# A twelve-stage decoder kernel: the two-way attention stage is written anew, with the gate weights folded into the value weights

## What is computed

```
Q_char = x @ Wq_c.T + bq_c;   K_sub  = ctx @ Wk_s.T + bk_s;  V_sub  = ctx @ Wv_s.T + bv_s
char2sub = softmax(Q_char @ K_sub.T / sqrt(128)) @ V_sub
Q_sub  = ctx @ Wq_s.T + bq_s; K_char = x @ Wk_c.T + bk_c;    V_char = x @ Wv_c.T + bv_c
sub2char = softmax(Q_sub @ K_char.T / sqrt(128)) @ V_char
gate = sigmoid(concat(char2sub, sub2char) @ Wg.T + bg)
out  = gate * char2sub + (1 - gate) * sub2char
```

## Time and profile before

| | |
|---|---|
| three runs, median (lowest to highest) | 1545.04 us (1542.69 to 1550.32) |
| the profiled execution: its own time, its span | 1544.58 us, 1542.8 us |
| mean granted TensorE clock, whole span | 0.947 |
| TwoWay with its LayerEnd | 177.2 to 245.6 us of the span |
| granted clock in that stretch | 0.83 |

### The profile page before, as it was taken

How to read it: one execution, slowest core, us unless ns; L and a number is a source line. 1 busy time by engine, 2 the same in 40 slices (tenths; PEclk the granted TensorE clock), 3 DMA queues, 4 the chain that set the end, 5 groups by cost and what they waited for, 6 DMA issues and landing times.

```text
span 1542.8 us, 24060 instructions
## 1 busy us (share of the span) xinstructions
PE 1311.6 (85%) x8965; PEld 835.4 (54%) x9015; DVE 942.9 (61%) x2189; ACT 668.5 (43%) x1896; POOL 398.4 (26%) x326
## 2 busy tenths in 40 slices
PE   7999866887877788777987379899898999999997
PEld 4666653555655533324564345556565666566664
DVE  2556566776665589986756867555764555633334
ACT  4555322556565486633642036322244555422222
POOL 1333102543432168835100252000101333300000
PEclk9999978999999998879998699999999999999999
DMA  9000000000000055520002200000000000000000
GB/s 392 3 1 2 0 1 1 1 1 1 1 1 1 21 129 126 127 59 2 2 1 96 124 1 2 1 1 0 1 2 1 1 1 1 1 1 1 0 0 14
DMA packets 13260, 43.29 MB, mean 28 GB/s; under 512 B 1760, under 2 KB 3936, under 8 KB 12512
## 3 DMA queue, kind: packets, MB, share of 16 engines
q1 hardware_dynamic: 13152, 41.84, 8.5%
HBM read 41.19 MB, written 0.66 MB: 27 GB/s over the span
## 4 chain that ended last, share of the span: by engine, by line
PE 67%; DVE 18%; ACT 6%; issue 4%; POOL 3%; DMA 1%; DVEq 0%; SPq 0%; POOLq 0%; ACTq 0%
PE PS L1071 6%; PE PS L641 6%; PE PS L1056 5%; PE PS L1057 5%; PE PS L325 4%; DVE PS L2120 4%; PE PS L357 3%; PE PS L337 3%; PE PS L707 3%; PE PS L298 2%; PE PS L306 2%; PE PS L366 2%; PE PS L300 2%; DVE arena L2127 2%; PE PS L319 2%
## 5 line engine op out<-in xcount | busy, mean ns | idle before, releaser
L549 POOL TENSOR_TENSOR arena<-arena,small 128x768 f32<-128x768 f32 (+1 forms) x64 | 107.7, 1683 | 226.5 <-DVE small L492 117.6
L877 DVE TENSOR_REDUCE arena<-PS 128x2 f32<-128x512 f32 (+1 forms) x192 | 108.8, 609 | 53.5 <-PE PS L635 52.4
L804 ACT ACTIVATE arena<-PS 128x512 f32<-128x512 f32 (+1 forms) x192 | 92.2, 532 | 107.2 <-PE PS L641 107.2
L1160 DVE TENSOR_TENSOR arena<-arena,PS 128x512 f32<-128x512 f32 x82 | 56.4, 687 | 115.9 <-ACT arena L1093 115.8
L1093 ACT ACTIVATE arena<-PS 128x512 f32<-128x512 f32 x82 | 49.0, 597 | 166.0 <-PE PS L1057 166.0
L1927 PE MATMUL PS<-arena,w_consts 128*128 128x512 f32 x128 | 84.7, 751 | 32.7 <-DVE arena L2127 29.4
L429 ACT ACTIVATE arena<-PS,small 128x256 f32<-128x256 f32 (+1 forms) x256 | 110.6, 452 | 0.0
L641 PE MATMUL PS<-arena 32*128 32x256 f32 (+1 forms) x768 | 97.5, 370 | 13.9 <-DVE arena L877 9.3
L635 PE MATMUL PS<-arena 32*128 32x256 f32 (+1 forms) x768 | 94.6, 371 | 2.4 <-DVE arena L877 1.6
L500 DVE COPY arena<-PS 128x768 f32<-128x768 f32 (+1 forms) x64 | 69.5, 1086 | 34.6 <-PE PS L337 34.5
L2171 POOL TENSOR_TENSOR arena<-arena 128x512 f32<-128x512 f32 x64 | 80.3, 1269 | 36.6 <-DVE PS L2120 28.1
(11 more groups left out here) (398 smaller groups left out, 3019.4 us busy)
## 6 DMA issues: line engine op xcount, KB each, us to landing
arena<-rows SPq DMA_DIRECT2D x32, 512.0 KB, 4.9
w_last<-in_last SPq DMA_DIRECT2D x1, 8260.0 KB, 22.3
w_rest<-in_rest SPq DMA_DIRECT2D x1, 6463.5 KB, 38.0
w_last<-in_first SPq DMA_DIRECT2D x1, 4532.5 KB, 21.5
w_last<-in_first SPq DMA_DIRECT2D x1, 2176.0 KB, 10.4
w_last<-in_mid SPq DMA_DIRECT2D x1, 768.0 KB, 4.3
X<-in_x SPq DMA_DIRECT2D x1, 512.0 KB, 4.7
CT<-in_ctxT SPq DMA_DIRECT2D x1, 512.0 KB, 11.0
```

The costliest lines, as they stand in the source:

```text
L549: g.tensor_tensor(p, p, ri, ALU.mult).then_inc(self.pn_done.sem, 1)
L804: a.activation(self.PT[:, q % 8, :], PS[:, 3 + q % 3, 0:2 * n], ACT.Exp).then_inc(self.e_done.sem, 1)
L877: v.tensor_reduce(dst, src, AX.X, ALU.max, negate=True).then_inc(self.mx_done.sem, 1)
```

## The change

TwoWay is rewritten, and its LayerEnd works in two groups:

- The value weights of direction i get 128 more columns, the product of the value weights and the direction's half of the gate weights; five small matmuls at the stage's start make this product and the matching bias (L1493 to L1497 of the changed kernel), and ACT copies them behind the plain value weights (L1508, L1509). Each value row then carries 256 numbers: value and gate share. So the matmul with the gate weights, the copy of outputs for it and its bias in each batch go.
- The transposed weights are now the stationary operand and the values the moving one, so the outputs have tokens on partitions (L1574: 8 matmuls of 256 columns in place of 4). The transposes of the result go.
- The weights stay undivided. ACT scales direction 1's output by 1/sum as it copies it (L1633), DVE scales direction 0's in the step that adds or subtracts the two (L1671). The division of 256 x 256 weights goes.
- Queries, keys and values read CT and XT themselves; the copies to CB and XB go. One direction's source makes its queries and keys into one bank, and ACT adds the bias to both (L1517, L1518). ACT in place of DVE copies the transposed weights (L1621).
- All four batches are written out, with no hardware loop.
- `early=True`: six tiles are normed between batch 2 and the last mixing step of batch 3; 8 + 5 filler matmuls stand on PE in place of 14.
- The fields `led` and `lead` are never set, so the branches on them do nothing: `lead_tensor` and `lead_scalar` run at the stage's start.
- The stage's weights take 0.4 MB more in the second of the two loads of the "first" weights.

```diff
-    def __init__(self, c, w, bq, bk, bv, wg, nbg):
+    def __init__(self, c, wq, wk, wv, wvt, bq, bk, bv, bvc, wg, bg):
...
+    def projections(self, pe, b, ctx, bank):
+        own = c.CT if ctx else c.XT
+        src = own[:, b * S:(b + 1) * S]
+        pe.matmul(c.PS[:, bank, 0:256], self.wq[:, i, :], src, start=True, stop=True)
+        pe.matmul(c.PS[:, bank, 256:512], self.wk[:, 1 - i, :], src, start=True, stop=True)\
+            .then_inc(self.qk_done.sem, 1)
+    def lead_tensor(self, pe):
+        c.wait_weights(pe, self)
+        for i in range(2):
+            pe.matmul(PS[:, 4, i * P:(i + 1) * P], self.wvt[:, i, :], self.wg[:, i, :], start=True, stop=True)
+        pe.matmul(PS[:, 4, 256:384], self.bvc[:, 0:1].to_broadcast([P, P]), self.wg[:, 0, :], start=True, stop=False,
+        pe.matmul(PS[:, 4, 256:384], self.bg.to_broadcast([P, P]), c.ident, start=False, stop=True, skip_group_check=True)
+        pe.matmul(PS[:, 4, 384:512], self.bvc[:, 1:2].to_broadcast([P, P]), self.wg[:, 1, :], start=True, stop=True,
+        self.projections(pe, 0, True, 2)
+        pe.wait_ge(self.x_ready.sem, self.x_ready.at(0, 1 if self.led else 2))
+        self.projections(pe, 0, False, 5)
...
+        def outputs(b):
+            pe.wait_ge(self.v_ev.sem, self.v_ev.at(b, 2))
+            if b:
+                pe.wait_ge(self.d_ready.sem, self.d_ready.at(b - 1, 1))
+            pe.wait_ge(self.pt_ev.sem, self.pt_ev.at(b, 2))
+            for i in (1, 0):
+                for t in range(2):
+                    for kt in range(2):
+                        ins = pe.matmul(PS[:, 6 + i, t * 256:t * 256 + 256],
+                                        self.PT[:, i, kt * 256 + t * P:kt * 256 + t * P + P],
+                                        self.V[b % 2][:, i, kt, :], start=(kt == 0), stop=(kt == 1), skip_group_check=True)
+                ins.then_inc(self.o_done.sem, 1)
+        values_of(0)
+        scores(0)
+        queries_keys(1)
+        values_of(1)
+        for b in range(B):
+            turns(b)
+            if b + 1 < B:
+                scores(b + 1)
+            else:
+                keep_warm(c, pe, 4, 4)
+            if b + 2 < B:
+                queries_keys(b + 2)
+            outputs(b)
+            if b + 2 < B:
+                values_of(b + 2)
+        self.end.transposes(pe, 0)
+        keep_warm(c, pe, 4, 8)
...
+        def batch(b):
             for i in range(2):
+                a.wait_ge(self.t_done.sem, self.t_done.at(b, i + 1))
+                if b and i == 0:
+                    a.wait_ge(self.o_done.sem, self.o_done.at(b - 1, 2))
+                a.activation(self.PT[:, i, :], PS[:, i, :], ACT.Copy).then_inc(self.pt_ev.sem, 1)
...
+                if b + 1 < B:
+                    exps(b + 1, i)
+                if b + 2 < B:
+                    queries_keys(b + 2, i)
+            if b + 1 == B:
+                self.end.root(a, 0)
+            a.wait_ge(self.o_done.sem, self.o_done.at(b, 1))
...
+                ins = a.activation(self.BG[:, t, :], PS[:, 7, t * 256:t * 256 + 256], ACT.Copy,
+                                   scale=self.ri[b % 2][:, 1, t:t + 1])
+            ins.then_inc(self.b_ready.sem, 1)
+            a.wait_ge(self.d_ready.sem, self.d_ready.at(b, 1))
+            a.activation(self.G, self.DG[:, :, P:2 * P], ACT.Exp, scale=-1.0).then_inc(self.g_exp.sem, 1)
...
+        def mixed(b):
+            r = self.ri[b % 2]
+            v.wait_ge(self.b_ready.sem, self.b_ready.at(b, 1))
+            v.wait_ge(self.o_done.sem, self.o_done.at(b, 2))
+            for lo, op in ((P, ALU.add), (0, ALU.subtract)):
+                for t in range(2):
+                    ins = v.scalar_tensor_tensor(self.DG[:, t, lo:lo + P], PS[:, 6, t * 256 + lo:t * 256 + lo + P],
+                                                 r[:, 0, t:t + 1], self.BG[:, t, lo:lo + P], ALU.mult, op)
+            ins.then_inc(self.d_ready.sem, 1)
...
+        for b in range(B):
+            if b + 1 < B:
+                maxima(b + 1)
+            if b:
+                finish(b - 1)
+            if b + 1 == B:
+                self.end.early_stats(v)
+                self.end.tiles(v, 0)
+            mixed(b)
+            if b + 2 < B:
+                values_of(b + 2)
+            if b + 1 < B:
+                sums(b + 1)
+            gates(b)
+        finish(B - 1)
...
-            s.end = LayerEnd(c, s.z_ready, last=i == len(names) - 1, early=isinstance(s, (Attention, NarrowAttention, LocalLayers, Mamba, BitLinear)),
+            s.end = LayerEnd(c, s.z_ready, last=i == len(names) - 1, early=isinstance(s, (Attention, NarrowAttention, LocalLayers, Mamba, BitLinear, TwoWay)),
```

More of the change, by code:

```diff
@@ L226, in scalar @@
         self.root(a, g)
+        if self.lead:
+            self.lead.lead_scalar(a)
         if self.turned:
@@ L232, in tensor @@
         if self.turned:
-            keep_warm(self.c, pe, self.spare, 5 if len(self.groups) == 2 else 14)
+            if self.lead:
+                self.lead.lead_tensor(pe)
+            else:
+                keep_warm(self.c, pe, self.spare, 5 if len(self.groups) == 2 else 14)
             self.transposes(pe, len(self.groups) - 1)
@@ L1502, in values_of @@
                 for t in range(2):
[L1503 to L1512, removed]
+                    ins = pe.matmul(PS[:, 2 + i, t * 256:t * 256 + 256], self.Q[:, i, t * P:(t + 1) * P],
@@ L1568, in source, with exps @@
-        def source(it, d):
-            if d:
-                a.wait_ge(self.v_done.sem, self.v_done.at(it, 2, d - 1))
-            a.activation(self.CB, c.CT[:, bass.ds(it * S + d * S, S)], ACT.Copy)
-            a.activation(self.XB, c.XT[:, bass.ds(it * S + d * S, S)], ACT.Copy).then_inc(self.src_ready.sem, 1)
-        def keys(it, d):
+        if not self.led:
+            self.lead_scalar(a)
+        def exps(b, i):
+            a.wait_ge(self.mx_done.sem, self.mx_done.at(b, i + 1))
+            if b and i == 0:
+                a.wait_ge(self.t_done.sem, self.t_done.at(b - 1, 2))
+            for t in range(2):
+                ins = a.activation(self.Pr[:, i, t * 256:t * 256 + 256], PS[:, 2 + i, t * 256:t * 256 + 256], ACT.Exp,
+                                   bias=self.nm[:, i, t:t + 1], scale=1.0, accum_out=self.ss[:, i, t:t + 1])
+            ins.then_inc(self.e_done.sem, 1)
@@ L1581, in batch @@
             for i in range(2):
-                a.wait_ge(self.mx_done.sem, self.mx_done.at(it, i + 1))
-                for t in range(2):
-                    ins = a.activation(self.Pr[:, i, t * 256:t * 256 + 256], PS[:, 6 + i, t * 256:t * 256 + 256],
-                                       ACT.Exp, bias=self.nm[:, i, t:t + 1], scale=1.0,
-                                       accum_out=self.ss[:, i, t:t + 1])
-                ins.then_inc(self.e_done.sem, 1)
-            if more:
-                keys(it, 1)
@@ new lines, in batch @@
+            for t in range(2):
+                ins = a.activation(self.BG[:, t, :], PS[:, 7, t * 256:t * 256 + 256], ACT.Copy,
[3 more added lines that the diff above has]
+            a.activation(self.G, self.DG[:, :, P:2 * P], ACT.Exp, scale=-1.0).then_inc(self.g_exp.sem, 1)
+        exps(0, 0)
+        queries_keys(1, 0)
+        exps(0, 1)
+        queries_keys(1, 1)
@@ L1607, in vector @@
+        for b in range(B):
+            batch(b)
     def vector(self, v):
@@ new lines, in finish, with sums @@
+            v.tensor_tensor(c.Z[:, 2 * b:2 * b + 2, :], self.G, self.BX, ALU.add).then_inc(self.z_ready.sem, 1)
+        def sums(b):
+            v.wait_ge(self.e_done.sem, self.e_done.at(b, 2))
+            link(v.reciprocal(self.ri[b % 2], self.ss))
+        values_of(0)
+        maxima(0)
+        values_of(1)
+        sums(0)
+        for b in range(B):
+            if b + 1 < B:
+                maxima(b + 1)
+            if b:
+                finish(b - 1)
[5 more added lines that the diff above has]
+                values_of(b + 2)
+            if b + 1 < B:
+                sums(b + 1)
+            gates(b)
```

256 lines of the change are left out of this document (103 added, 153 removed).

## The result

| | before | after |
|---|---|---|
| median of seven runs each | 1545.04 us (1542.15 to 1551.02) | 1534.6 us (1532.63 to 1537.06) |
| profiled execution: own time, span | 1544.58, 1542.8 | 1536.69, 1534.6 |
| x ready behind TwoWay | 245.56 | 231.28 |

The ratio of the times is 0.9929, 95% interval 0.9907 to 0.9951: 10.4 us faster by the medians, 7.6 to 14.4 by the interval. The forecast was 1533, its range 1529 to 1540.

A forecast was written before the change was run, and what follows sets the result against it. A ring of dependent steps was taken as TwoWay's bound, PE after the change. x ready at 233.5 instead of 245.56 saves 12.0 us: span 1530.8, execution 1532.6, plus 0.46 for the median: 1533, range 1529 to 1540.

The forecast's parts named there:

- The ring and its end: In TwoWay, PE bounds batches 0 and 1 at 9.55 us each, and batch 2's outputs end at 216.0.
- The slack of 1.2 us: In each batch, PE has 4.35 us of work while DVE and ACT need about 3.1 to copy the weights.
- The sixteen weight loads at nothing: In each batch's outputs, weight loads cost nothing, each lying under the 0.21 us record before it.
- The start: At TwoWay's start, clock at 1.2 GHz until about 181.1, 0.85 us a matmul, values starting at about 183.5.
- rival 3: More gain: clock up already at 177.4 (1.9 us less), 1 us less in hand-overs; gain 15, 1530; chance 0.07.
- The repeated-column matmuls at 0.22 each: At TwoWay's start, they cost as any 128-column matmul; at worst as 256 columns, +1.3 us for three.
- The tail: From batch 2's outputs at 216.0, DVE bounds TwoWay's end, and x is ready at 233.5.
- about 1.4 on this item alone: In TwoWay's tail, six early tiles add 4.5 us to the path and replace 6.7 by 3.6 behind the last sum.
- The price weighed: For mixing in four steps of 128 numbers, the profile row's 1.12 us was used over the skill's estimate of 1.03.
- Its like would take 1532.6: Whole kernel: a profiled execution like the one of 1544.58 us would take 1532.6, with span 1530.8.
- Rival 2: Clock takes part back: 1.2 GHz stretches at L0f's start and in the PE-bound part; gain 6.7, 1538; chance 0.20.
- L0f longer by more than 2 us: A sign that the prediction is wrong: the stage behind TwoWay grows by more than 2 us.

The follow-up runs named there:

- after_scores_twice: Changed kernel with the four score matmuls of batches 1 and 2 issued twice; 1540.73 us in one run, TwoWay 57.77 us.
- before_order: Kernel before, written out, gate steps and result transposes moved into the next batch, outputs double buffered; median 1538.08 us, ratio 0.9943.
- after_divided: Changed kernel with DVE dividing the weights before PE turns them, and no scalings by 1/sum; median 1543.08 us, ratio 0.9982.
- before_warm: Kernel before with filler matmuls on PE in the wait ahead of each batch's result transposes; median 1546.18 us, ratio 1.0002.
- before_written_out: Kernel before with the hardware loop over its first two batches written out, nothing else; 1548.9 us in one run, TwoWay 67.2 us.
- before_later: Kernel before with 24 fillers in place of 14 behind TwoWay, shifting later stages; median 1553.28 us, ratio 1.0029.
- before_again: Kernel before, unchanged, profiled a second time; 1544.38 us.
- after_late: Changed kernel with all eight tiles normed behind TwoWay's last sum, early group undone; median 1533.07 us, ratio 0.9927 against the kernel before.
- after_again: Changed kernel, unchanged, profiled a second time; 1533.39 us, TwoWay 54.31 us.
- after_led: Changed kernel with led and lead set, so TwoWay's first matmuls run inside L0a's LayerEnd; median 1530.67 us, ratio 0.9879 against the kernel before.
- late_led: Changed kernel with TwoWay's first matmuls in L0a's LayerEnd and all eight tiles normed late; median 1530.71 us, ratio 0.9883 against the kernel before.
- after_warm_tail: Changed kernel with 22 fillers in place of 5 at TwoWay's end; median 1536.54 us, ratio 0.9909 against the kernel before.

## Why the prediction was nearly right

**The ring and its end: right.** The forecast was two batches of 9.55 and outputs of batch 2 ending 32.5 us behind the start of the values (183.5 to 216.0). Measured: 9.60 and 9.50 in the windows, and 181.05 to 213.55 on the chain, 32.5. after_scores_twice shows that PE is the bound, before_order that the gate chain had been. In one batch (197.8 to 207.3) DVE was busy for 6.93 us and ACT for 5.82, where 7.4 and 6.5 had been costed. The slack of 1.2 us held too: ACT's copies, in the row below, ended at 199.53, and PE came to the queries and keys that wait for them at 200.57, 1.0 us later. after_divided shows what a step of DVE would have cost there.

```profile
198.44 1.09 ACT L1621 ACTIVATE arena<-PS 128x512 f32<-128x512 f32 x2 [0.50 <-PE PS L1563]
```

**The sixteen weight loads at nothing: right.** The outputs took 3.47 for 16 records, 0.217 each.

**The start: mis-sized.** The term was "0.85 a matmul" until 181.1, and values at 183.5. Measured 181.05, 2.4 us earlier: the clock was 1.00 (0.57 in before), so the five small matmuls took 1.10 and not 2.15, and the context's two projections 0.88 and not 1.70: 1.9 us, which was rival 3's first term. The rest is a start 0.2 earlier and x's projections, which ran beside ACT's copies and not ahead of them. How far it is the change's doing is open: PE's work ahead of 177.2 is the same, and the clock there was 1.00 in all eight profiles with the changed stage but also in before_warm, before_written_out and before_later, and 0.57 to 0.62 in before, before_again and before_order. Some 1.2 us of the stage's gain (before_written_out) may be that.

**The repeated-column matmuls at 0.22 each: right** (L1496: 0.22 for its two records).

**The tail: right.** 17.5 forecast, 213.55 to 231.28 = 17.7 measured. The remark that the early six tiles lose "about 1.4 on this item alone" was wrong: they don't cost their whole 4.5 us on the path, since without them batch 3's mixing would wait for PE until 220.24 (after_late), only 2.75 us ahead of 222.99. Behind the last sum they save 3.1 (3.8 us in after, 6.9 in after_late), so they cost nothing (54.3 and 54.65).

**The price weighed: the row.** The mixing took 1.14 and 1.05 us in after, the row of before said 1.12. The estimate of 1.03 from the Trainium skill ("VectorE: DVE Perf Modes", the TRN2 errata) is under both. Two such groups of four differ from it by 0.13 in all, too little to matter.

**The sum of the stage** was 12.0 and is 14.1; the difference is the start's.

**"Its like would take 1532.6", taking all later stages as fixed: this step failed.** L0f to L2a took 6.7 and 3.4 us more in the two profiles of after than in those of before. Rival 2 had this effect and about this size, but not the mechanism: no stretch at 1.2 GHz fell into the PE-bound part, and the repeated columns were cheap. L0f did start cold (0.58), but PE's wait for ACT took that up, much as the prediction's argument against rival 2 had it (other engines' work beside L0f's first matmuls), and 205 us later nothing of it was left. The Trainium skill's rule on the clock ("TensorE: Matmul & The Clock Gate", "What's actually happening") had that cold start, and the trace agrees. The sign of being wrong "L0f longer by more than 2 us" came up in part: L0f with L1a took 2.8 us more, but by a later stretch. What the runs show in place of the fixed lengths: stretches at 1.2 GHz fall elsewhere within L0f+L1a, L1x, L1f and L2a from kernel to kernel (before_warm, before_later) and between executions of one program (after and after_again). What makes them fall so, and which shift is dear and which cheap, stays open.

How much of the change's own gain is given back is less sure than the profiles make it look. By the profiled executions' times 7.9 us are left, by the medians 10.4, since the profile of after was 2.1 us dearer than its median and that of before 0.5 cheaper. The interval of the total, 7.6 to 14.4 us, even holds the stage's whole 14.1, and three other kernels kept all of theirs: after_led with 18.5 us in the stage and 18.7 by its ratio, late_led with 18.1 and 18.1, after_warm_tail with 14.2 and 14.1. A loss behind the stage is clear of noise only in before_warm, and in after_divided, where the stage was 7.6 us shorter and the total at most 5.4.

So two errors cancelled in part: the stage was 2.1 us better than summed, the rest 3.7 worse by the medians. That the total came within 1.6 us of 1533 is to that extent luck.

## What to carry to other kernels

When no engine is full, look on the chain for the one step that holds the next batch's first instruction, and move it behind a batch's worth of work before making any step cheaper: here that order alone gave 10.2 of the 14.1 us. Once PE is the bound, each wait of PE on DVE shows at once (6.4 us for a division), and a stage's lead belongs under the LayerEnd before it (4.4 us). Judge an edit by its own stage's window and by medians of the whole against the old kernel run beside it, never by the span of one profile, since the stages behind, unchanged, moved here by up to 10.5 us.

## What the runs showed of the chip that was not expected

- Fillers on PE raised the granted clock of two batches from 0.79 to 1.00 and shortened the stage by 3.5 to 3.8 us (5.0 with the stage's start, which was fast in that profile too), and the total stayed (ratio 1.0002): the stages behind took 8.0 more.
- L0f's start at 0.58 in place of 1.00 cost nothing: its first two matmuls took 1.25 us longer, and the next two began no later behind x, since they wait for ACT.
- 0.8 us of delay with no other edit went with 3.9 us more in L1x, at 0.57 where 1.00 had been. Whether the delay did it isn't shown.
- Two executions of one program differ by 2.0 us in a stage of 50 (L1f), by the clock alone: 15 against 25 records in 5.26 us of busy PE.
- A stationary operand that repeats one column costs PE as any other, 0.22 us for 128 columns in f32.
